# An equivariant graph network on one core: the first turn of q ahead of the scalar sums, and a message pair between the turn of y and the vector products

## The reference

```python
xj = x[col]; s, v = split(xj)                        # features of the edge's other node
m0 = (s @ W_ss) * dist + (v . r) @ W_vv + s @ L_s    # message, scalars
m1 = (s @ W_sv) * r + (v @ W_vs) * dist + v @ L_v    # message, vectors
a0, a1 = split(segment_sum([m0, m1], row))           # sum over the edges of a node
u0 = einsum('nu,nv,uvw->nw', xs, a0, U_ss) + einsum('nui,nvi,uvw->nw', xv, a1, U_vv)
u1 = einsum('nu,nvi,uvw->nwi', xs, a1, U_sv) + einsum('nui,nv,uvw->nwi', xv, a0, U_vs)
x = layernorm(x + x + merge(u0 + xs @ Lu_s, u1 + xv @ Lu_v))
```

## Time and profile before

| | |
|---|---|
| median of 3 runs | 6655.41 us (6651.92 to 6660.94) |
| the profiled execution | 6649.59 us, its span 6647.9 us |
| granted TensorE clock, mean | 0.918 |
| busy: PE, DVE, ACT, POOL | 82%, 82%, 56%, 77% |
| DMA | 1380.94 MB, mean 208 GB/s |
| first stage | up to about 2250 us |
| second stage | about 2250 to 4860 us |
| third stage | from there to the end |

### The profile page before, as it was taken

The page is one execution under the profiler, slowest core; times in us unless marked ns, Lnnn a source line. Parts: engine busy times, 40 slices in busy tenths (PEclk is TensorE's granted clock), DMA queues, the critical chain, the costliest instruction groups (busy, mean ns, idle before and its releaser), DMA issues.

```text
span 6647.9 us, 144690 instructions
## 1 busy us (share of the span) xinstructions
PE 5431.9 (82%) x52095; PEld 4342.4 (65%) x52095; DVE 5458.2 (82%) x7292; ACT 3710.3 (56%) x11578; POOL 5133.5 (77%) x4006
## 2 busy tenths in 40 slices
PE   5566666666666499999999999999589999999998
PEld 3445444554545377777777777777467777777777
DVE  6777777777778589999999999989378888888988
ACT  2333333333333366666666666666267777777776
POOL 2777777777777568888888888877778888888887
PEclk7778888778788799999999999999799999999999
DMA  7888888888886278888888888888422232222222
GB/s 226 257 256 260 256 257 256 258 253 258 260 257 204 92 236 275 278 272 272 275 275 273 272 278 265 271 264 269 153 88 94 95 103 94 94 96 102 94 95 76
DMA packets 681145, 1380.94 MB, mean 208 GB/s; under 512 B 106047, under 2 KB 487661, under 8 KB 654447
## 3 DMA queue, kind: packets, MB, share of 16 engines
q1 hardware_dynamic: 527695, 1090.23, 52.2%
q0 software_dynamic: 152736, 281.45, 12.5%
HBM read 587.20 MB, written 784.08 MB: 206 GB/s over the span
## 4 chain that ended last, share of the span: by engine, by line
PE 36%; SPq 14%; DVE 13%; POOL 13%; DMA 9%; ACT 8%; issue 6%; POOLq 0%; DVEq 0%; ACTq 0%
PE node_ps L1368 11%; PE prods_ps L1306 6%; DMA rec<-edge_recs 5%; DVE upd L1092 5%; ACT onehot L1714 5%; POOL q L737 4%; PE prods_ps L1325 4%; SPq L353 4%; POOL q L772 3%; SPq L379 3%; PE s_ps L1222 3%; DMA table<-tab 2%; DVE zs L1043 2%; POOL picks_sb L763 2%; PE prods_ps L1309 2%
## 5 line engine op out<-in xcount | busy, mean ns | idle before, releaser
L654 POOL DMA_INDIRECT slots<-pay,slot_all x3136 | 3246.8, 1035 | 1037.0 <-issue 813.1
L1714 ACT ACTIVATE onehot<-node_iota,msgs 128x125 f32<-128x125 f32 x3400 | 1028.1, 390 | 121.9 <-POOLq L698 121.9
L1368 PEld LDWEIGHTS node_ps<-msgs,onehot 128*125 128x125 f32 x6800 | 932.0, 188 | 139.4 <-ACT onehot L1720 83.1
L1368 PE MATMUL node_ps<-msgs,onehot 128*125 128x160 f32 x6800 | 980.8, 303 | 35.9 <-ACT onehot L1720 25.3
L1092 DVE TENSOR_REDUCE upd<-work 125x48 f32<-125x3072 f32 x300 | 1004.1, 3347 | 6.8
L1079 DVE TENSOR_TENSOR work<-prods_ps,yv 125x1024 f32<-125x1024 f32 x800 | 931.3, 1217 | 52.0 <-PE prods_ps L1310 51.1
L737 POOL TENSOR_TENSOR q<-xt,yv 125x3072 f32<-125x3072 f32 x100 | 547.7, 5477 | 302.1 <-PE turn_ps L1355 285.1
L1500 ACT COPY picks_sb<-s_ps 125x512 f32<-125x512 f32 x392 | 229.9, 586 | 938.6 <-PE s_ps L1204 706.3
L1190 PE MATMUL prods_ps<-bucket_onehot,after_bf 128*128 128x500 bf16 x392 | 174.9, 446 | 667.5 <-DVE bucket_onehot L909 666.9
L1222 PE MATMUL m_ps<-win,picks_sb 125*128 125x160 f32 x3136 | 654.2, 336 | 68.6 <-ACT pay L1515 61.7
L1222 PEld LDWEIGHTS m_ps<-win,picks_sb 125*128 125x128 f32 x3136 | 519.4, 215 | 145.6 <-ACT pay L1515 91.2
(11 more groups left out here) (268 smaller groups left out, 13339.8 us busy)
## 6 DMA issues: line engine op xcount, KB each, us to landing
msgs<-slots SPq DMA_DIRECT2D x200, 1428.0 KB, 6.4
slots<-zero SPq DMA_DIRECT2D x183, 1386.0 KB
win<-table SPq DMA_DIRECT2D x784, 160.0 KB
picks<-picks_sb SPq DMA_DIRECT2D x196, 512.0 KB
picks_sb<-picks SPq DMA_DIRECT2D x196, 512.0 KB
table<-tab SPq DMA_DIRECT2D x200, 350.0 KB
slots<-pay,slot_all POOLq DMA_INDIRECT x3136
spill_in<-spill_sums SPq DMA_DIRECT2D x200, 80.0 KB, 6.1
```

The lines of the kernel that those rows point to most:

```text
L654: g.indirect_dma_start(out=slots[layer][:, :], out_offset=bass.IndirectOffsetOnAxis(ap=slot_all[:, j:j + 1], axis=0), in_=pay[q][:, j - UB ...
L1368: te.matmul(node_ps[0:HM, 0:D], onehot[:, j, :], msgs[b][:, j, 0:D], start=(j == 0), stop=False)
L1714: last = ac.activation(onehot[:, j, :], node_iota[:, :], ACT.Square, bias=msgs[b][:, j, LOCAL:LOCAL + 1], scale=-1.0)
```

## The change

TensorE issues turn_q(0) before scalar_sums instead of behind it, and message(1, 0) behind turn_y instead of between the two turns of q. ACT copies that message pair before the scalar and vector sums instead of behind them. Only the second stage is touched.

```diff
                 message(0, 3)
                 sum_edges()
+                turn_q(0)
                 scalar_sums()
-                turn_q(0)
-                message(1, 0)
                 turn_q(1)
                 turn_y()
+                message(1, 0)
                 vector_products()
                 linear()
@@ ACT
                 turned_q(1)
                 turned_y()
+                paid(1, 0)
                 scalars_out()
-                paid(1, 0)
```

## The result

The changed kernel takes 6619.08 us, the median of its runs (6612.07 to 6627.28), against 6655.41 (6651.92 to 6660.94). The ratio is 0.9942, its 95% interval 0.9931 to 0.9953: **36 us or 0.6% faster**, inside the range of 6576 to 6640 and 24 us behind the forecast of 6595. It is outside the forecast's own 6580 to 6612, and nearer to the 6628 of rival A. The profiled execution is the one of 6619.08 us, its span 6617.3.

A forecast was written before the change was run, and what follows sets the result against it. TensorE was taken as the bound, 96% busy in 24.72 us steps and waiting on q_t's second copy. Gains of 52 (71 steps), 6 (early) and 2 (last 21) made 60 us: 6595 us predicted, range 6576 to 6640.

The forecast's parts named there:

- rival A: POOL is the next bound: scatter collisions can't go below 1.2 us a step, floor 24.4, time 6628; chance 0.17.
- Steps 1 to 3: TensorE's chain: turn at 0.37, scalar sums beside copy and distances, message covering second copy; 0.73 us less per step.
- steps 2 and 3: New TensorE chain with old lengths, message pair behind turn of y: vector products at 4.06 instead of 4.79 us.
- step 4: Other engines keep up: VectorE still waits 0.58 us for lin, POOL's floor is 23.2 us a step; 0 lost.
- step 5: Sum over the stage, 52 + 6 + 2 = 60 us; DMA paces the last 21 steps, which gain 2, lower end 0.
- the early six steps: Second stage's steps before the 71, without messages: 1.17 us less each, at most 7, taken as 6.
- B: A second path, ACT's one-hots or lin, is as long; only the early six steps gain, 6649 us; chance 0.11.
- D: DMA engines 87% busy at 23.99 us steps make loads late from the start: pace 25.08, 6681 us; chance 0.05.
- C: First turn, heading TensorE's queue, is exposed to VectorE's late addition: 0.1 to 0.4 us a step slower, 6676; chance 0.05.

The follow-up runs named there:

- e1: Kernel before with only the first turn of q moved ahead of the scalar sums, message pair left in place: 6661.86 us, ratio 1.0010.
- e3: Changed kernel with the first of four rows of scalar sums (16 of 64 matmuls) ahead of the first turn: 6600.68 us, ratio 0.9914.
- e12: Changed kernel with a row of scalar sums first and, in the last 27 steps, SP's zeros ahead of the store wait and windows: 6577.68 us.
- e11: Kernel before, with SP issuing x_mid, records and zeros ahead of the store wait and windows in its last 27 steps: 6646.88 us, ratio 0.9987.
- e10: Changed kernel, with SP issuing x_mid, records and zeros ahead of the store wait and windows in the last 27 steps: 6594.57 us, ratio 0.9912.
- e5: Changed kernel with only the table stores of the last 25 steps issued by ACT on its own DMA queue: 6609.16 us, ratio 0.9927.
- e4: Changed kernel with all second-stage table stores issued by ACT on its own DMA queue: 6630.84 us, ratio 0.9959.

## Why the prediction was right or wrong

**Right: the mechanism.** Steps 1 to 3 hold in sign and order: the turn waits for line 1064 and starts at 0.36 (0.37 said), the scalar sums lie beside copy and distances, the wait of line 1336 for the copy is gone, and the message's copy ahead of the scalar copy costs nothing. The gain was foreseen as 71 x 0.73; it is 71 x 0.54 = 38 by regular steps, and 32.6 in the profiled execution.

**Luck: the time inside the range.** The mechanism gave 6580 to 6612, and 6619 is behind it. It lies in the stated range because that had been stretched to the 6628 of rival A, whose mechanism the steps refute (below). The profiled execution is 29.5 us behind the 6589.6 that was forecast for it: 19.4 of that lie in the 71 steps, 12.4 in the 21, which no rival foresaw, and 3.0 in the early ones. A first stage that happened to be 5.8 shorter hides a part of it.

**Mis-sized: two hand-offs in steps 2 and 3**, together 0.17 of the missing 0.19. The turn was given 0.48 up to the next work on PE; in front of the scalar sums it is 0.58 (3599.34 to 3599.92; 0.57 in e1 and e3). The message pair was given 0.55, as the 0.83 from its start to the second turn less a wait of 0.28; it takes 0.64 (0.65 in e1, and in e3). The 0.28 was my own arithmetic from the copy's end, and the row has no wait in brackets. By the 0.64, the wait in it was 0.83 - 0.64 = 0.19. Where a length is found by subtraction, a second place where the same work stands without a wait gives it directly. The copy of q_t is covered with 0.14 to spare (0.07 said), so what the message takes longer delays the products in full.

**Right: step 4, nobody else.** h still waits, 0.77 where 0.58 was said, the difference being the same late products. POOL followed at 24.18 and at 23.95, so rival A is false. Why it could is now a row and not an argument: POOL's busy time for the same 1344 instructions is 1427.86 us in the earlier trace rows, 1396.09 after and 1376.55 in e12, that is 0.45 less a step where the step is 0.54 shorter, and then 0.27 less where it is 0.23 shorter. The holds on its scatters are what shrinks, as the step does: their mean goes from 1060 ns in the earlier trace rows to 1031 after and 1014 in e12, while its products stay at 1078 to 1081 and its idle time in front of the scatters at 315 to 317 us.

**Wrong: step 5, the last 21 steps**, +2 said, -10.4 measured. "The pace is already 25.08" took a mean for a pace: of those 21 steps before, 17 took 24.72 and one 29.68. The wait for the store had been building up behind a slack, and a faster TensorE uses that up sooner: in the kernel before, the time from a store to its windows grows from 3.1 us (store at 4114) to 15.6 (at 4336), and the step of 29.68 comes right behind that; in the changed kernel steps are late from the fourth on. "A faster TensorE only waits longer" has a floor of 0 for the gain; what it left out is that a wait which reaches TensorE also costs clock (28.73, 32.28 and 29.40 us for the three steps with a granted clock below 1.00, with waits of 2.9, 3.5 and 2.6 us for the copy of q_t in them; 17.9 us above 24.18 in all). The lower bound should have been a loss, not 0.

**Too high: the early six steps**, 6 said, 3.0 measured (1.8 between e11 and e10). A regular one goes from 21.91 to 21.03, 0.88 instead of 1.17: the missing 0.29 is the wait of line 1306 for VectorE's zs, which grew from 1.35 to 1.67 a step. One of the six took 22.20 at a granted clock of 0.92.

**The rivals.** B is false, D too (up to 4107, at a DMA share of 0.86, SP waits for table stores 3.1 us at line 490 and 3.6 at line 498; e12 runs all its steps at 23.95 with a share of 0.87). C did not decide here: the addition ends at 0.31. But e1 shows its mechanism at work at 24.87 us a step, and the changed kernel is 0.08 us away from it if the collision came each time. It was worth more than the twentieth that I gave it.

What stays open: five us in the 71 steps of the changed kernel's profiled execution (1722.77 against the 1717.72 of e10, which differs only behind them). Most of it is one step of 28.16 us, in which PE has an idle time of 2.30 us that the profile ascribes to nothing, and a granted clock of 0.94. It may not be chance alone: the same step of e5 takes 29.36 us, with an idle time of 2.03 at the same line, but 24.36 in e10. The cause stays open.

```profile
2759.68 0.31 PE L1164 MATMUL turn_ps<-ident,res 125*96 125x125 f32 x1 [2.30 <-issue]
```

## What to carry to other kernels

Two moves that are worth nothing alone can be worth half a microsecond a step together: draw the whole chain from the moved work to its consumer, and look for what still stands in it. Work put at the head of an in-order queue meets its producer's lateness without cover; sixteen matmuls in front of it bought back 0.23 us of 0.36. Before crediting a stretch with "the DMA sets the pace, nothing to lose", read its steps one by one: a mean over steps that are mostly on time hides a wait that is growing behind them. The cheap cure was another order in the issuing queue: what nobody waits for goes behind the store that somebody waits for, and not in front of it.

## What the hardware showed beside that

VectorE's product into q3 (both inputs in SBUF) takes 2.12 us on average in e1 and 1.32 in the changed kernel:

```profile
L1056 DVE TENSOR_TENSOR q<-xt,yv 125x1024 f32<-125x1024 f32 x71 | 150.4, 2118 | 0.0
```

It starts at 3728.14, POOL's product at 3728.13, and it is VectorE that is held; in the earlier trace rows a scatter of POOL is held by VectorE's product that had started before it. The Trainium skill, "SBUF — State Buffer", section "Who interferes with whom", says that the order of issue decides who is blocked; the trace agrees in these two cases. In the third, h, the row puts VectorE's start 0.20 before POOL's, and h is held all the same; no run here settles that one.

A queue of its own did not make a DMA early: from the store of 0.39 MB to the windows that wait for it, 10.9 us beside 2.9 MB on the other queue, 16.0 behind them. The Trainium skill, "DMA: Bandwidth & Descriptors", section "Issuing engines are not separate DMA queues", says that DMAs of different engines interleave on the same 16 DMA engines; the trace agrees. It also calls the time to initiate a DMA usually small relative to the DMA itself. Here the two parts of one store take 0.35 and 4.44 us to issue on SP, and a pair of windows 4.93; both long ones come within 6 us behind 1.4 MB or more on the same queue, but no run isolates why. With 0.78 for two issues on ACT, each step of e4 is 0.20 longer.

The granted clock stayed at 1.00 in regular steps, each with an idle wait of 0.30 us, was 0.84 in the step with the wait of 3.53 and 0.94 in the one with 2.30; matmuls of line 1306 then take 0.41 us instead of 0.27, and 0.27 again before the same step ends. These are the two levels of the clock, 1.2 and 2.4 GHz. The early steps show both too: one takes 21.02 us at 1.00 in the changed kernel and 23.50 at 0.85 in e3. What the engine did before that fall I have not traced, and early steps of single executions are therefore no measure of an edit.
